# Masked cross attention: scores taken once with queries on partitions, exponentials turned by TensorE

## The chip, the cores and the metric

The kernel runs on one NeuronCore of a Trainium2 chip. The metric is the device time of one launch in microseconds. Before the change it is 2520.6 us (median of three runs, 2520.56 to 2532.2).

## The reference, cut to what matters

A small Perceiver of two layers over x [16, 64, 256] and a context [16, 1601, 256]: cross attention, an RWKV block, a mixture of experts; then cross attention with a mask and biases, differential attention, and a routed block. Only the second cross attention (layer `L1_xattn`) changes:

```python
q = split_heads(query @ Wq.T + bq)      # query: layer norm of x, 16 heads of 16
k = split_heads(key @ Wk.T + bk)        # key, value: the context, 1601 rows
v = split_heads(value @ Wv.T + bv)
scores = einsum('bhqd,bhkd->bhqk', q, k) / 4 + mask * -1e9
ctx = einsum('bhqk,bhkd->bhqd', softmax(scores), v)
x = x + ctx @ Wo.T + bo
```

## The kernel before

Six stages run one after another (A to F), with a barrier behind each. A and D are the two cross attentions, and both use `cross_attention`; D passes a mask. The work is cut into 32 groups: a group is one of the 16 batches and one half of its heads, eight heads as four pairs, j = 0 to 3. A pair has 32 channels and 128 columns of queries (64 of each head). The 1601 keys are 13 tiles of 128 (the last has 65) and four chunks of 512 (the last has 65).

Per group TensorE computes scores twice. First with queries on partitions (`score`, L536: 96 rows, since keys and queries are stacked as high and low fp32r halves; 16 matmuls into a ring of three PSUM banks), of which VectorE takes the maximum (`largest`; with a mask by the operation at L691, which adds the scaled mask). The negated maximum is turned onto rows (`turn_max`, L544) and placed in rows 96 to 127 of the stacked queries (`place_max`). Then again with keys on partitions (`scoresT`, L570: per key tile four matmuls of 128 rows, which subtract the maximum through these rows), with a mask one more matmul of 512 columns ahead of them (L566), ScalarE's exp from PSUM to SBUF (L648), and `values` (L584: 8 fp32 matmuls of 32 output rows per tile, four column groups, into `OUT`).

Keys are projected by `k_unit` (six fp32r matmuls per chunk) and values by `v_unit` (twelve per unit). ScalarE writes the high half of the keys (`k_hi`), VectorE the low half (`k_lo`), and 24 DMAs per group on SyncE's queue copy both into the stack `k_stack` (`keys`, L404); twelve more per batch bring the queries (`queries`, L391). GpSimd splits context, queries and mask.

The order is written out by hand: for each group g and key tile t TensorE does `scoresT(g, t)` and, at the slots in `K_SLOT`, `V_SLOT` and `S_SLOT`, a projection for the next batch or a score for group g+1; `values` run in pairs two tiles behind; `spread_sums` (L553) of group g-1 stands at slot 5, and VectorE's `finish` (L723 to L730) behind it. ScalarE and VectorE follow the same loops. Ahead of the attention lies the query stage (L231, L240), in which ScalarE fills rows of `k_stack` with ones (L247).

Of the kernel before, what the change touches and what calls it, by code (L numbers as in the profile page):

```python
# [8 lines left out]
F32 = mybir.dt.float32  # L9
# [61 lines left out]
class Chip:  # L71


    def __init__(self, nc):
        self.nc, self.used = nc, []

    def sem(self, name):
        self.used.append(self.nc.alloc_semaphore(name))
        return self.used[-1]
# [175 lines left out]
class Cross:  # L255


    def __init__(self, nc, chip, ctx, ctxT, tag):
        def sb(name, shape, dt=F32):
            return ctx.enter_context(nc.sbuf_tensor(name + tag, shape, dt))  # L260
        self.nc, self.ctxT = nc, ctxT
        self.raw = [sb(f"raw{i}", [P, HALVES, BANK]) for i in range(2)]
        self.xh, self.xl = sb("ctx_hi", [P, HALVES, KPAD], F32R), sb("ctx_lo", [P, HALVES, KPAD], F32R)
        self.stack = [sb(f"k_stack{i}", [P, 4, KPAD], F32R) for i in range(2)]
        self.raw_in = [chip.sem(f"raw_in{i}{tag}") for i in range(2)]
        self.ctx_hi_done, self.ctx_ready = chip.sem("ctx_hi_done" + tag), chip.sem("ctx_ready" + tag)

# [61 lines left out]
def cross_attention(nc, chip, cross, qT, attnT, wk, wv, bk, bv, mask, late, late_in, tag):  # L329
# [7 lines left out]
    with ExitStack() as ctx:  # L337
# [336 lines left out]
        def _(dve):  # L674
# [69 lines left out]
            for g in range(GROUPS):  # L744
                m, h = g // 2, g % 2
                for t in range(KT):
                    if t == MAX_SLOT and g + 1 < GROUPS:
                        negate(g + 1)
                        place_max(g + 1)
                    if t in K_SLOT and m + 1 < NB:  # L750
                        k_lo(m + 1, 4 * h + K_SLOT[t])
                    if t in S_SLOT and g + 1 < GROUPS:
                        for k in S_SLOT[t]:
                            largest(g + 1, k)
                    if t == SUM_SLOT and g:
                        finish(g - 1)
            finish(GROUPS - 1)

# [1026 lines left out]
def cross_stage(nc, chip, dram, layer, tag, mask):  # L1785

    with ExitStack() as ctx:
        def sb(name, shape, dt=F32):
            return ctx.enter_context(nc.sbuf_tensor(name + tag, shape, dt))
        qT, cross = sb("qT", [P, HALVES, TOK]), Cross(nc, chip, ctx, dram["ctxT"], tag)  # L1790
        bq, bk, bv = sb("bq", [P, HALVES]), sb("bk", [P, HALVES]), sb("bv", [P, HALVES])
        wo, bo, late_in = cross.raw[0][:, :, 0:D], cross.raw[1][0:1, 0, 0:D], chip.sem("late_in" + tag)
        w_step = chip.sem("w_step" + tag)
# [3 lines left out]
        with ExitStack() as ctx2:  # L1797
            split = [[ctx2.enter_context(nc.sbuf_tensor(n + tag, [P, HALVES, D], F32R))
                      for n in (w + "_hi", w + "_lo")] for w in ("wk", "wv")]
            with ExitStack() as ctx3:  # L1800
                y, yT, wq, wk, wv = [ctx3.enter_context(nc.sbuf_tensor(n + tag, [P, *s], F32)) for n, s in
                                     (("y", [NT, D]), ("yT", [HALVES, TOK]), ("wq", [HALVES, D]),
                                      ("wk", [HALVES, D]), ("wv", [HALVES, D]))]
                weights = [(t[:, :, :], chan(dram[layer + n])) for t, n in
                           ((wk, "Wk"), (wv, "Wv"), (wq, "Wq"))]
                if mask is not None:
                    weights += [(t[:, :], dram[layer + n]) for t, n in
                                ((bq, "bq"), (bk, "bk"), (bv, "bv"))]

                def early_loads(sp):  # L1810
                    cross.load(sp, 0, 0)
                    cross.load(sp, 0, 1)

                def early_splits(pool, loaded):
                    nc.gpsimd.memset(cross.xh[:, :, KEYS:KPAD].bitcast(F32), 0.0)
                    nc.gpsimd.memset(cross.xl[:, :, KEYS:KPAD].bitcast(F32), 0.0)
                    if mask is None:
                        for b in (bq, bk, bv):
                            nc.gpsimd.memset(b[:, :], 0.0)
                    pool.wait_ge(loaded, 16 * len(weights))  # L1820
                    for i, (w, (hi, lo)) in enumerate(zip((wk, wv), split)):
                        nc.gpsimd.tensor_copy(hi[:, :, :], w[:, :, :]).then_inc(w_step, 1)
                        pool.wait_ge(w_step, i + 1)
                        nc.gpsimd.tensor_tensor(lo[:, :, :], w[:, :, :], hi[:, :, :].bitcast(F32), ALU.subtract)
                    cross.split(pool, 0, 0)
                    cross.split(pool, 0, 1)
                norm_stage(nc, chip, chip.x, y, lambda h, q: yT[:, h, BANK * q:BANK * q + BANK], weights,
                           more_sync=early_loads, more_pool=early_splits, tag=tag)
                query_stage(nc, chip, cross, yT, wq, bq, 1.0 if mask is None else 0.25, qT, tag)
            cross_attention(nc, chip, cross, qT, qT, *split, bk, bv, mask, late, late_in, tag)  # L1830
        output_stage(nc, chip, qT, wo, None if mask is None else bo, late_in, len(late), tag)


# [82 lines left out]
```

## Time and profile before

| | |
|---|---|
| median of the runs | 2520.6 us |
| profiled execution | 2541.2 us |
| its span | 2539.4 us |
| TensorE busy, matmuls | 2204.7 us (87%) |
| VectorE / ScalarE / GpSimd busy | 1252.5 / 1011.8 / 614.2 us |
| mean granted clock of TensorE | 0.904 of 2.4 GHz |

The second cross attention's groups run from 1447.5 to 2317 us of the span. Busy times of TensorE overlap, since matmuls are pipelined: what an instruction costs its queue is read from its start to the next one's start. An fp32 matmul appears as two records, an fp32r matmul or a transpose as one. "x4" in a timeline is four records merged into one row; the time beside it runs from the first start to the last end.

### The profile page before, as it was taken

How to read it: one execution, taken by the hardware profiler on the slowest of the kernel's cores; microseconds unless marked ns; L12 is line 12 of the kernel's file. 1: busy time of each engine (PE TensorE's matmuls, PEld its weight loads, DVE VectorE, ACT ScalarE, POOL GpSimd, SP SyncE). 2: the span in 40 equal slices, each digit the busy share in tenths (PEclk: the TensorE clock that was granted, in tenths of full speed). 3: DMA queues.
4: the chain of work that ended last, by engine and by line, in shares of the span. 5: the costliest groups of instructions: out<-in, count | busy, mean ns of one | idle time of the engine just before them, and what ended most of it. 6: DMA issues, size and time to landing. Idle time of an engine off the chain costs nothing. (4 is left out here: it accounts for less than half of the span.)

```text
span 2539.4 us, 60278 instructions
## 1 busy us (share of the span) xinstructions
PE 2204.7 (87%) x24656; PEld 1817.9 (72%) x24656; DVE 1252.5 (49%) x2909; ACT 1011.8 (40%) x2180; POOL 614.2 (24%) x473
## 2 busy tenths in 40 slices
PE   5799999999999984194997799999999999998774
PEld 3687878878887862164896578888888888886453
DVE  3354544545445437823313345545545545543685
ACT  3244444444444423220322334444444444442581
POOL 3122222332222000021001353334444334410010
PEclk9799999999999957595998799999999999997766
DMA  4445555555555401005131555656556556540000
GB/s 119 114 120 132 137 120 133 126 137 136 131 126 128 105 17 41 0 1 190 67 119 50 136 125 140 145 135 146 139 137 145 136 139 144 139 98 23 13 1 23
DMA packets 166867, 267.52 MB, mean 105 GB/s; under 512 B 70713, under 2 KB 86210, under 8 KB 166594
## 3 DMA queue, kind: packets, MB, share of 16 engines
q1 hardware_dynamic: 166594, 263.66, 42.2%
q8 instruction: 198, 3.24, 0.6%
q14 instruction: 75, 0.61, 0.1%
HBM read 98.70 MB, written 1.05 MB: 39 GB/s over the span
## 5 line engine op out<-in xcount | busy, mean ns | idle before, releaser
L648 ACT ACTIVATE exp_d<-scoresT_d 128x512 f32<-128x512 f32 (+1 forms) x416 | 248.3, 597 | 274.2 <-PE scoresT_d L570 271.8
L691 DVE CUSTOM_DVE_ANT_0 scores_d<-scores_d,mask_scaled_d 128x512 f32<-128x512 f32 (+1 forms) x512 | 281.1, 600 | 145.8 <-PE scores_d L536 142.7
L695 DVE TENSOR_REDUCE max_parts_a<-scores_a 128x1 f32<-128x512 f32 (+1 forms) x512 | 263.4, 565 | 157.3 <-PE scores_a L536 157.3
L648 ACT ACTIVATE exp_a<-scoresT_a 128x512 f32<-128x512 f32 (+1 forms) x416 | 247.9, 596 | 214.5 <-PE scoresT_a L570 213.2
L570 PE MATMUL scoresT_a<-q_stack_a,k_stack_a 128*128 128x128 f32 (+1 forms) x1664 | 261.9, 283 | 0.9 <-DVE q_stack_a L712 0.9
L570 PEld LDWEIGHTS scoresT_d<-q_stack_d,k_stack_d 128*128 128x128 f32 (+1 forms) x1664 | 244.3, 187 | 24.1
L570 PEld LDWEIGHTS scoresT_a<-q_stack_a,k_stack_a 128*128 128x128 f32 (+1 forms) x1664 | 233.1, 198 | 28.3 <-issue 3.6
L570 PE MATMUL scoresT_d<-q_stack_d,k_stack_d 128*128 128x128 f32 (+1 forms) x1664 | 227.6, 259 | 0.0
L536 PE MATMUL scores_a<-k_stack_a,q_stack_a 96*128 96x512 f32 (+1 forms) x512 | 178.9, 404 | 40.2 <-issue 20.3
L679 DVE SCALAR_TENSOR_TENSOR k_lo_d<-project_d,bk_d,k_hi_d 128x512 fp32r<-128x512 f32 (+1 forms) x128 | 81.1, 635 | 258.0 <-ACT k_hi_d L631 258.0
L679 DVE SCALAR_TENSOR_TENSOR k_lo_a<-project_a,bk_a,k_hi_a 128x512 fp32r<-128x512 f32 (+1 forms) x128 | 80.8, 633 | 255.5 <-ACT k_hi_a L631 255.5
L284 POOL CAST ctx_hi_a<-raw_a 128x1024 fp32r<-128x1024 f32 x64 | 54.6, 853 | 586.4 <-PE project_a L110 504.7
L566 PE MATMUL scoresT_d<-pick_d,mask_hi_lo_d 128*128 128x512 f32 (+1 forms) x416 | 186.4, 448 | 0.8 <-issue 0.8
L536 PE MATMUL scores_d<-k_stack_d,q_stack_d 96*128 96x512 f32 (+1 forms) x512 | 171.2, 387 | 12.2 <-DMA k_stack_d<-k_hi_d 6.2
L284 POOL CAST ctx_hi_d<-raw_d 128x1024 fp32r<-128x1024 f32 x64 | 54.7, 855 | 470.1 <-PE project_d L110 379.1
L584 PE MATMUL values_a<-exp_a,v_a 128*32 128x64 f32 x6656 | 141.4, 228 | 1.5
L584 PEld LDWEIGHTS values_a<-exp_a,v_a 128*32 128x32 f32 x6656 | 107.0, 113 | 48.7 <-issue 39.2
L640 ACT ACTIVATE v_a<-project_a 128x512 f32<-128x512 f32 (+1 forms) x112 | 63.4, 566 | 187.6 <-PE project_a L110 187.4
L584 PE MATMUL values_d<-exp_d,v_d 128*32 128x64 f32 x6656 | 136.3, 222 | 1.7 <-ACT exp_d L648 0.2
L584 PEld LDWEIGHTS values_d<-exp_d,v_d 128*32 128x32 f32 x6656 | 102.6, 109 | 47.8 <-issue 38.7
L536 PEld LDWEIGHTS scores_a<-k_stack_a,q_stack_a 96*128 96x128 f32 x512 | 89.3, 199 | 55.8 <-issue 21.8
L108 PE MATMUL project_a<-wv_hi_a,ctx_hi_a 128*128 128x256 f32 (+1 forms) x416 | 126.4, 304 | 1.1 <-DVE k_lo_a L679 1.1
(370 smaller groups left out, 4849.6 us busy)
## 6 DMA issues: line engine op xcount, KB each, us to landing
k_stack_a<-k_hi_a SPq DMA_DIRECT2D x256, 128.0 KB
k_stack_d<-k_hi_d SPq DMA_DIRECT2D x256, 128.0 KB
raw_a<-in_ctxT SPq DMA_DIRECT2D x48, 512.0 KB, 4.2
raw_d<-in_ctxT SPq DMA_DIRECT2D x48, 512.0 KB, 5.0
w_c<-in_L_ffn_W SPq DMA_DIRECT2D x23, 1024.0 KB, 9.5
k_stack_a<-k_hi_a SPq DMA_DIRECT2D x256, 72.2 KB, 2.1
k_stack_d<-k_hi_d SPq DMA_DIRECT2D x256, 72.2 KB
k_stack_a<-k_lo_a SPq DMA_DIRECT2D x128, 128.0 KB
```

The lines of the kernel that those rows point to most:

```text
L108: nc.tensor.matmul(out, sh, mh, start=start, stop=False)
L284: self.nc.gpsimd.tensor_copy(self.xh[:, :, cols], self.raw[j % 2][:, :, 0:w]).then_inc(self.ctx_hi_done, 1)
L536: nc.tensor.matmul(SC[at % 3][:, 0:even(chunk)], qs[m % 2][0:96, 4 * h + j, :], stack[h][0:96, j, cols], start=True, stop=True).then_inc(s ...
L566: nc.tensor.matmul(bank[0:r, :], mb[m % 2][:, cols], pick[:, :].rearrange("p (a c) -> p a c", a=1).to_broadcast([P, 4, P]), start=True, st ...
L570: ins = nc.tensor.matmul(bank[0:r, P * j:P * j + P], stack[h][:, j, cols], qs[m % 2][:, 4 * h + j, :], start=not masked, stop=True, skip_g ...
L584: ins = nc.tensor.matmul(OUT[PW * j:PW * j + PW, h, T * a:T * a + T], v[m % 2][0:r, PAIRS * t + 4 * h + j, 16 * a:16 * a + PW], eT[at % RI ...
L640: nc.scalar.activation(pairs[:, :, 0::2, :], PJ[at % 2][0:r, 0:D * tiles].rearrange("p (i a c) -> p i a c", a=2, c=16), ACT.Copy).then_inc ...
L648: nc.scalar.activation(eT[at % RING][0:r, :], ST[at % 2][0:r, :], ACT.Exp).then_inc(exp_done, 1)
L679: nc.vector.scalar_tensor_tensor(kl[:, cols], PJ[at % 2][:, 0:even(chunk)], bk[:, h:h + 1], kh[:, cols].bitcast(F32), ALU.add, ALU.subtrac ...
L691: nc.vector.tensor_tensor_reduce(SC[at % 3][:, 0:w], SC[at % 3][:, 0:w], mf[m % 2][:, BANK * chunk:BANK * chunk + w], 1.0, NEG, ALU.add, A ...
L695: nc.vector.reduce_max(parts[:, j, chunk:chunk + 1], SC[at % 3][:, 0:w], AX.X).then_inc(score_free, 1)
```

## The change

Stage D gets its own function, `cross_by_rows`; stage A keeps `cross_attention`. In it:

- Keys are kept once in fp32 (`keys`, two buffers, one for each half), written by ScalarE or VectorE; `k_stack`, its fill with ones, the low halves, and the copies of keys and queries by DMA are gone.
- Scores are computed once per group, in four rounds (one per chunk) of four fp32 matmuls with 32 rows each, on partitions 32j, into four banks `SC[j]`. A round waits until VectorE has read all four banks of the round before.
- VectorE adds the mask and takes the maximum, and writes the masked scores to `maps` in SBUF. ScalarE takes exp over `maps` in place, four pairs by two pieces (1024 and 577 columns), with the negated maximum as bias. The mask matmul, `turn_max` and `place_max` are gone.
- TensorE turns `maps` tile by tile (four transposes of 128x128 per tile into two banks `TP`). ScalarE moves tiles 0 to 6 to SBUF, VectorE tiles 7 to 12. `values`, the sums and `finish` stay, the latter behind slot 9.
- Projections use one bank (`PJ`) in the steady state, three ahead of the first group. From slot 7 on VectorE keeps them, before that ScalarE.

The diff, cut to its core:

```diff
+K_AT = {1: 0, 4: 1, 7: 2, 10: 3}
+V_AT = [{3: 0, 6: 1, 9: 2, 12: 3}, {3: 4, 6: 5, 9: 6}]
+ROUND_AT = {0: 0, 2: 1, 4: 2, 6: 3}
+SUM_AT = 9
+LATE = 7
...
+            def scores(g, chunk):
+                m, h, w = g // 2, g % 2, cross.width(chunk)
+                if chunk == 0 and h == 0:
+                    pe.wait_ge(q_ready, m + 1)
+                wait_kept(pe, ("k", m, 4 * h + chunk))
+                after(pe, score_free, ROUND["score", g, chunk, 0])
+                for j in range(4):
+                    own = slice(PW * j, PW * j + PW)
+                    ins = nc.tensor.matmul(SC[j][:, 0:w], qs[m % 2][own, h, :],
+                                           keys[h][own, BANK * chunk:BANK * chunk + w], start=True, stop=True)
+                ins.then_inc(scored, 1)
+            def turn(g, t):
+                at, r = KT * g + t, rows(t)
+                if t in (0, CUT // P):
+                    pe.wait_ge(exp_done, 8 * g + (4 if t == 0 else 8))
+                wait_moved(pe, at - 2)
+                for j in range(4):
+                    ins = nc.tensor.transpose(TP[at % 2][0:r, P * j:P * j + P], maps[g % 2][:, j, P * t:P * t + r],
+                                              chip.ident)
+                ins.then_inc(turned, 1)
...
+            for g in range(GROUPS):
+                m, h = g // 2, g % 2
+                for t in range(KT):
+                    if t == 0 and g:
+                        values(g - 1, KT - 1)
+                    turn(g, t)
+                    if t in ROUND_AT and g + 1 < GROUPS:
+                        scores(g + 1, ROUND_AT[t])
+                    if t in K_AT and m + 1 < NB:
+                        k_unit(m + 1, 4 * h + K_AT[t])
+                    if t in V_AT[h] and m + 1 < NB:
+                        v_unit(m + 1, V_AT[h][t])
+                    if t == SUM_AT and g:
+                        spread_sums(g - 1)
+                    if t and t % 2 == 0:
+                        values(g, t - 2)
+                        values(g, t - 1)
...
+            def exp(g, piece, j):
+                cols, b = (slice(CUT, KEYS) if piece else slice(0, CUT)), g % 2
+                act.wait_ge(max_ready, g + 1)
+                nc.scalar.activation(maps[b][:, j, cols], maps[b][:, j, cols], ACT.Exp,
+                                     bias=low[:, b, j:j + 1]).then_inc(exp_done, 1)
...
+            for g in range(GROUPS):
+                m, h = g // 2, g % 2
+                for t in range(LATE):
+                    move(g, t)
+                    if t == 0 and g:
+                        keep_out(g - 1)
+                    if t in K_AT and m + 1 < NB:
+                        keep_k(m + 1, 4 * h + K_AT[t])
+                    if t in V_AT[h] and m + 1 < NB:
+                        keep_v(m + 1, V_AT[h][t])
+                if g + 1 < GROUPS:
+                    for i in range(8):
+                        exp(g + 1, i // 4, i % 4)
...
+                nc.vector.tensor_tensor_reduce(
+                    maps[b][:, j, cols], SC[j][:, 0:w], mf[m % 2][:, cols] if masked else none[:, 0:w], 1.0, NEG,
+                    ALU.add, ALU.max, parts[:, j, chunk:chunk + 1]).then_inc(score_free, 1)
...
+            for g in range(GROUPS):
+                m, h = g // 2, g % 2
+                for t in range(KT):
+                    if t >= LATE:
+                        move(g, t)
+                    if t in ROUND_AT and g + 1 < GROUPS:
+                        for j in range(4):
+                            largest(g + 1, ROUND_AT[t], j)
+                        if ROUND_AT[t] == 3:
+                            negate(g + 1)
+                    if t >= LATE and t in K_AT and m + 1 < NB:
+                        keep_k(m + 1, 4 * h + K_AT[t])
+                    if t >= LATE and t in V_AT[h] and m + 1 < NB:
+                        keep_v(m + 1, V_AT[h][t])
+                    if t == SUM_AT and g:
+                        finish(g - 1)
...
-        qT, cross = sb("qT", [P, HALVES, TOK]), Cross(nc, chip, ctx, dram["ctxT"], tag)
+        qT, cross = sb("qT", [P, HALVES, TOK]), Cross(nc, chip, ctx, dram["ctxT"], mask is None, tag)
...
-            cross_attention(nc, chip, cross, qT, qT, *split, bk, bv, mask, late, late_in, tag)
+            attend = cross_attention if mask is None else cross_by_rows
+            attend(nc, chip, cross, qT, qT, *split, bk, bv, mask, late, late_in, tag)
```

## Rows read from the trace of the kernel before

**Rows 1.** Table of stretches (start:end, length, busy per engine, granted clock, DMA)

```profile
1447.50:1500.40 52.90, 44.26 (x489) 37.75 (x490) 19.55 (x55) 17.81 (x31) 21.87 (x14) 0.88 0.57 138
1500.40:2291.50 791.10, 785.74 (x10351) 667.08 (x10351) 414.99 (x1276) 354.06 (x621) 307.26 (x191) 1.00 0.58 136
```

**Rows 2.** TensorE's timeline (start, duration, engine, line): sums of two groups

```profile
1856.56 0.41 PE L553 MATMUL scores_d<-out_copy_d,const 128*128 128x64 f32 x2
...
2268.49 0.29 PE L553 MATMUL scores_d<-out_copy_d,const 128*128 128x64 f32 x1
```

**Rows 3.** TensorE's timeline, steady group: its sums and work behind it

```profile
1801.31 0.63 PE L553 MATMUL scores_d<-out_copy_d,const 128*128 128x64 f32 x4
...
1803.88 0.68 PE L536 MATMUL scores_d<-k_stack_d,q_stack_d 96*128 96x512 f32 x2
1804.48 0.65 PE L584 MATMUL values_d<-exp_d,v_d 128*32 128x64 f32 x32
1805.07 0.50 PE L566 MATMUL scoresT_d<-pick_d,mask_hi_lo_d 128*128 128x512 f32 x1
1805.41 0.56 PE L570 MATMUL scoresT_d<-q_stack_d,k_stack_d 128*128 128x128 f32 x4
1805.80 0.45 PE L108 MATMUL project_d<-ctx_hi_d,wk_hi_d 128*128 128x512 f32 x1
...
1807.25 0.39 PE L536 MATMUL scores_d<-k_stack_d,q_stack_d 96*128 96x512 f32 x1
```

**Rows 4.** TensorE's instructions by form, one group (xcount | busy us, mean ns)

```profile
L570 PE MATMUL scoresT_d<-q_stack_d,k_stack_d 128*128 128x128 f32 x48 | 6.7, 262 | 0.0
...
L536 PE MATMUL scores_d<-k_stack_d,q_stack_d 96*128 96x512 f32 x13 | 5.0, 421 | 0.0
```

**Rows 5.** Timeline and stretch: transposes in the differential stage; plain fp32 matmuls

```profile
2485.53 3.67 PE L1547 MATMUL ht_e<-const,gained_e 128*128 128x128 f32 x16 [5.16 <-DVE gained_e L1539]
...
2485.50:2489.20 3.70, 3.67 (x16) 3.27 (x16) 1.78 (x3) 1.80 (x3) 0.00 (x0) 0.50 0.00 0
...
1399.05 4.46 PE L231 MATMUL q_d<-yT_d,wq_d 128*128 128x512 f32 x10
```

**Rows 6.** VectorE's timeline: two masked reads, and finish of a group

```profile
1439.05 0.73 DVE L691 CUSTOM_DVE_ANT_0 scores_d<-scores_d,mask_scaled_d 128x512 f32<-128x512 f32 x1
...
1439.70 0.73 DVE L691 CUSTOM_DVE_ANT_0 scores_d<-scores_d,mask_scaled_d 128x512 f32<-128x512 f32 x1
...
1802.32 0.95 DVE L723 RECIPROCAL rec_d<-scores_d 128x128 f32<-128x128 f32 x1
...
1804.35 0.70 DVE L691 CUSTOM_DVE_ANT_0 scores_d<-scores_d,mask_scaled_d 128x512 f32<-128x512 f32 x1
```

**Rows 7.** Instructions by form: a copy on VectorE, exps on ScalarE

```profile
L1673 DVE COPY dT_e<-dt_e 128x512 f32<-128x512 f32 x16 | 11.0, 686 | 2.4 <-PE dt_e L1607 2.4
...
L648 ACT ACTIVATE exp_d<-scoresT_d 128x512 f32<-128x512 f32 x384 | 229.4, 597 | 268.2 <-PE scoresT_d L570 265.9
...
L961 ACT ACTIVATE e_b<-e_b 128x1024 f32<-128x1024 f32 x6 | 6.3, 1057 | 23.3 <-DVE e_b L881 20.0 <-DVE e_b L898 3.0
```

**Rows 8.** Timeline ahead of the first group [idle before <-releaser]

```profile
1394.10 11.51 ACT L247 ACTIVATE k_stack_d<-const 32x1602 fp32r<-32x1602 f32 x8 [0.27 <-PEq L131]
...
1403.54 0.75 DVE L240 TENSOR_SCALAR qT_d<-q_d,bq_d 128x512 f32<-128x512 f32 x1 [0.97 <-PE q_d L231]
...
1423.20 0.48 PE L108 MATMUL project_d<-ctx_hi_d,wk_hi_d 128*128 128x512 f32 x1
...
1430.10 1.26 ACT L631 ACTIVATE k_hi_d<-project_d,bk_d 128x512 fp32r<-128x512 f32 x2 [6.56 <-DMA k_stack_d<-k_hi_d]
...
1447.54 0.76 PE L566 MATMUL scoresT_d<-pick_d,mask_hi_lo_d 128*128 128x512 f32 x1 [0.83 <-issue]
```

**Rows 9.** Table of stretches, first cross attention: TensorE waits, and afterwards

```profile
565.80:569.20 3.40, 1.99 (x58) 1.53 (x57) 0.35 (x2) 1.62 (x4) 2.93 (x5) 1.00 0.68 152
569.20:572.70 3.50, 3.12 (x13) 3.02 (x14) 0.69 (x1) 0.00 (x0) 0.39 (x1) 0.51 0.53 119
```

More of the change, by code:

```diff
@@ L255, with __init__ @@
 class Cross:
-    def __init__(self, nc, chip, ctx, ctxT, tag):
+    def __init__(self, nc, chip, ctx, ctxT, stacked, tag):
         def sb(name, shape, dt=F32):
@@ L263, in __init__ @@
         self.xh, self.xl = sb("ctx_hi", [P, HALVES, KPAD], F32R), sb("ctx_lo", [P, HALVES, KPAD], F32R)
-        self.stack = [sb(f"k_stack{i}", [P, 4, KPAD], F32R) for i in range(2)]
+        self.stack = [sb(f"k_stack{i}", [P, 4, KPAD], F32R) for i in range(2)] if stacked else []
         self.raw_in = [chip.sem(f"raw_in{i}{tag}") for i in range(2)]
@@ L755, in _, with unit_order @@
                     if t == SUM_SLOT and g:
+                        finish(g - 1)
+            finish(GROUPS - 1)
+K_AT = {1: 0, 4: 1, 7: 2, 10: 3}
[3 more added lines that the diff above has]
+LATE = 7
+FIRST_UNITS = 15
+def unit_order():
+    order = [("k", 0, k) for k in range(4)] + [("v", 0, u) for u in range(7)] + [("k", 0, k) for k in range(4, 8)]
+    for m in range(1, NB):
+        for h in range(HALVES):
+            for t in range(KT):
+                if t in K_AT:
+                    order.append(("k", m, 4 * h + K_AT[t]))
+                if t in V_AT[h]:
+                    order.append(("v", m, V_AT[h][t]))
+    return {unit: i for i, unit in enumerate(order)}
```

260 lines of the change are left out of this document (added).

## The prediction

> **What bounds the kernel now.** I read four views, from coarse to fine. The table of stretches first: over the long stretch of the second cross attention TensorE is busy 785.74 of 791.10 us at a granted clock of 1.00, while VectorE has 414.99 and ScalarE 354.06 us of work [rows 1]. So nothing but TensorE's own queue sets the pace there, and a change pays by what it takes out of that queue, as long as no other engine becomes the next one. Second, two marks of the same matmul (the one that spreads the sums, slot 5 of a group): a pair of groups from 1801.31 to 1856.56 us takes 55.25 us, and fifteen groups from 1856.56 to 2268.49 take 411.93 us, so 27.46 us per group [rows 2, 3]. Third, the groups of TensorE instructions of one group: 48 full transposed-score matmuls beside four narrow ones, so 52 over 13 key tiles, each tile led by one mask matmul; 12 score matmuls of 512 columns (the window catches 13) and four narrow ones [rows 4]. Fourth, the timeline, for what each costs from its start to the next start, since the busy times overlap [rows 3]. From 1805.41 to 1805.80 four transposed scores take 0.39. A key unit, six matmuls of 512 columns, takes 1.45 (1805.80 to 1807.25), 0.24 each. A mask matmul, also 512 columns, takes 0.34 behind values (1805.07 to 1805.41) and I count 0.23 elsewhere. A pair of values tiles takes 0.59 (1804.48 to 1805.07), of which the records need 0.65-0.22=0.43 and the change of tile shape about 0.15.
>
> **What leaves TensorE, per group.** Mask: 7 x 0.23 + 6 x 0.34 = 3.65 us. Transposed scores: 13 x 0.39 = 5.1. First scores: two of them with the values switch behind take 0.60 (1803.88 to 1804.48), so 12 x 0.29 plus four narrow ones at 0.12 = 4.0. Turning of the maximum: about 0.35. Together 13.1 us.
>
> **What comes in.** (a) 52 transposes of 128x128 fp32. The trace has them in the differential stage: 16 in 3.67 us, of which the last one's own 0.42 is latency, so 0.217 us each, at a clock of 0.50 [rows 5]. It never shows one at the full clock. A plain fp32 matmul of 512 columns at the full clock takes (4.46-0.59)/9 = 0.43 us per record [rows 5], 0.84 ns a column, and the transpose at half clock 1.7 ns a column: the same cycles. I take 0.108 each, 5.6 us per group; the other end is 0.217, 11.3 us. (b) The mask matmul was also what stood between values and the next 128-row work; its extra 0.11 now falls on a turn, six times: 0.7. (c) Scores with 32 rows each on four row groups. fp32 has two records of 0.43 per matmul. If the four run beside one another, a round takes 0.86; if they don't, 3.44. Nothing in the trace splits rows. The nearest row splits columns: 32 values records take 0.43 us [rows 3], 14 ns apiece, while 64 columns at 0.84 ns are 54 ns alone, so four groups do run side by side there. I take 0.86 plus 0.2 for changing shape: 3 x 1.06 + 0.4 for the narrow round = 3.6. Together 9.9 us.
>
> The Trainium skill (TensorE: Matmul & The Clock Gate, Part 3) gives 3.07 times for four row tiles with 512 columns, not four times. No row here shows it. By it a round would be 8 x 0.43 / 3.07 = 1.12, and the sum some 6 us later.
>
> So TensorE's need falls from 27.46 to 24.3 us per group. Whether it gets that depends on the others.
>
> **VectorE's new chain.** Each round writes all four score banks, and the next round waits until VectorE has read all four: the ring of three single banks is gone. One masked read starts 0.65 after the one before [rows 6], so four take 2.6 and the hand-overs 0.2. It now writes maps to SBUF. The nearest PSUM to SBUF row, a copy of 512 columns, took 0.686 [rows 7], less than the 0.73 of a read as it is, so I keep 0.65 (0.70 would cost 5 us in all, 0.60 gain as much). TensorE's filler between rounds 0 and 1 is turn, key unit, turn: 0.43+1.45+0.43 = 2.3, so about 0.5 us of wait. Between 1 and 2 it is values, turn, value unit, turn: 0.74+0.43+1.43+0.43 = 3.0, and between 2 and 3 as much: covered. A group then runs: values and turn 0.75, round 0 to 1.8, round 1 at 4.65, round 2 at 8.75, round 3 done at about 13.2. From there VectorE does the narrow reads and the new maximum (1.2 us), then moves 7 to 12 at 0.69 each (that copy again), two or three kept units, and the finish of the old group, 1802.32 to 1804.35 = 2.03 [rows 6]. The finish is queued ahead of move 10, and turn 12 waits for move 10: about 10.2 us after round 3, while TensorE's own queue has brought it there after 10. Both ends together: 26.1 us with four value units, 24.6 with three; 25.4 on average, a saving of 2.05 per group. VectorE's work is some 17 us per group, so as a sum it does not bind; only its order does.
>
> **ScalarE** has 7 moves (0.597 each, by the exp of the same tile), 8 exps over SBUF (four of 1024 columns, which took 1.057 [rows 7], some 0.94 from start to start; four of 577, 0.54 in proportion), kept units and the output: about 14 of 25 us. The exps start when the maximum is ready, 1.2 to 2 us after round 3, and need 5.9; the next group's first turn comes 11 us after round 3. If that cover went, every us over it would be paid in each group.
>
> **Queues.** SyncE loses 24 key copies per group and 12 query copies per batch, so context and mask loads are never behind them. The mask load now waits for a read of group 2m-3, two groups ahead of its use. GpSimd loses two of its three mask steps and the query splits, and keeps the splits of the context; it only gets freer.
>
> **Ahead of the first group** and in its first two. Today: the ones' fill on ScalarE runs 1394.10 to 1405.61 and ends the query stage, whose last VectorE step is over at 1403.54+0.75 = 1404.3: 1.3 us go [rows 8]. Then ScalarE waits 6.56 us until the copies have left k_hi, and the first transposed score starts at 1447.54 [rows 8]. After: TensorE does keys, values and rounds without those waits. Key unit 4 starts at 1423.20 today [rows 8]; with four rounds ahead of it (3.6 us) it ends near 1428; ScalarE then has a table load, six exps and four kept units before the bank wait lets the first turn go, near 1436.4: 11 us earlier. The stretch from 1447.5 to 1500.4 lasts 52.90 at clock 0.88 [rows 1] for 1.4 groups, some 39 us at the steady pace. That excess of 14 is copies and splits arriving late; I give 10 of it back. The last two groups have no projections: there the reads chain costs 1 us more and the last group's moves 1 less.
>
> **Sum.** 30 x 2.05 = 61.5; + 10 + 11 + 1.3 = 84. Waits of 0.5 us may cost some clock: in the first cross attention a stretch with 1.99 of 3.40 us busy was followed by one at 0.51 [rows 9]. Each such 3.4 us stretch loses 1.7; I take off 8 us for five of them. Net 76. The profiled execution took 2541.2 us (span 2539.4), the median is 2520.6: 2465 there, x 2520.6/2541.2 = 2445 us.
>
> **Rivals.**
> A. *The four row groups do not run side by side.* A round costs 3.44+0.2, 2.6 more, three times per group, with VectorE waiting for the last: +8 per group, about 2690. Against it: the values rows.
> B. *The clock falls.* The turns are 5.6 of 25 us, with small waits around. Every transpose in the trace ran at 0.50 [rows 5], although always after an idle stretch. If a share f of the time were at half clock a group would last 25.4/(1-f/2); at f = 0.2 it eats the gain. At a third it is 30.5 per group and about 2600. That is the slower side, decided at f = 0.2. A transpose that stays at 0.217 ends near the same place (+5 per group).
> The skill's page on TensorE (Part 4, PE-mode transpose) says that transposes do not count as activity for the clock; if so, this rival is the one it speaks for. The trace can't tell, because all of its transposes follow a wait.
> C. *Lock step.* Round and read alternate with later hand-overs, or the finish pushes turns 10 to 12: 1.5 us more per group, 2490 to 2500; the gain mostly gone.
> D. *Better.* VectorE's order doesn't bind and TensorE gets its 24.3: 2410.
>
> **How the numbers follow.** Forecast 0.54, A 0.08, B 0.16, C 0.14, D 0.08. 8 in 10: from 2405 (D and the low bounds) to 2570, which leaves out A and most of B. This kernel can be told from no change at about 0.5%, 12.6 us. Faster: forecast, D and most of C, 0.74; same 0.05; slower 0.21.
>
> **What would show it.** A turn as four transposes 0.107 apart at clock 1.00; a round's eight records within 0.9 us; marks of the sums 25.4 apart on average; waits of TensorE for the masked reads near 0.5 per group, for the last moves near nothing; the first turn near 1436. Wrong if the clock row of the long stretch shows less than 0.9, if a round takes 2 us or more, or if ScalarE's exps end after the group's last turn.

## The result and the profile after

The changed kernel takes 2461.2 us (median of four runs, 2453.0 to 2464.2) against 2520.6; the ratio is 0.9753, with a 95% interval of 0.9712 to 0.9794. The profiled execution took 2461.6 us, its span is 2459.8.

The lengths in this part are read from TensorE's timeline in the same way for every kernel: the start of the first transpose (or first transposed score) of groups 0, 2 and 30, and of the last of all. A turn is the four transposes of one key tile. The pace is the difference between groups 2 and 30, divided by 28.

| second cross attention, us | before | after | difference |
|---|---|---|---|
| end of the query stage's last VectorE step to group 0 | 43.8 | 34.3 | -9.5 |
| groups 0 and 1 | 67.1 | 52.6 | -14.5 |
| groups 2 to 29 (pace) | 768.1 (27.43) | 721.4 (25.77) | -46.7 |
| group 30 to the last turn | 31.5 | 33.0 | +1.4 |

Together 69.3 us. The two profiled executions differ by 79.6: 11.4 more stand ahead of this stage, in code that is the same (the last step of the query stage ends at 1404.3 before [rows 8] and at 1392.9 here), and 1.1 comes back behind it. The profiled execution before was 20.6 us above its median, the one after 0.4 above its own. That is why the medians, 59.4 us apart, and not the two profiles are the measure. Of the 20 us, 11 stand ahead of the stage; no run shows where the others lie, and the 69.3 may hold some of them.

The table of stretches of the changed kernel, the columns as in [rows 1]:

```profile
1437.00:1490.00 53.00, 50.59 (x728) 38.51 (x727) 30.39 (x92) 27.93 (x42) 15.24 (x10) 1.00 0.18 48
1490.00:2240.00 750.00, 711.72 (x10524) 548.28 (x10524) 462.82 (x1344) 386.82 (x577) 198.10 (x130) 1.00 0.16 44
```

In the long stretch the clock stays at 1.00, as before, TensorE is busy 95% where it was 99% [rows 1], the moved data fall from 136 to 44 GB/s, and VectorE and ScalarE have more to do. Groups 0 and 1 ran at a lower clock before than they do now (before, then after):

```profile
1447.50:1514.80 67.30, 58.55 (x712) 49.97 (x712) 28.21 (x84) 24.42 (x42) 26.90 (x19) 0.91 0.56 133
1427.16:1479.70 52.54, 50.91 (x714) 38.84 (x714) 30.25 (x89) 27.80 (x41) 19.78 (x15) 0.96 0.22 61
```

At a mean clock of 0.91 some 6 of the 67 us are lost, at 0.96 some 2 of the 53: by this estimate about 4 of the 14.5 us come from the clock. The marks of the sums, to hold against [rows 2]:

```profile
1500.50 0.44 PE L979 MATMUL scores_d<-out_copy_d,const 128*128 128x64 f32 x3
...
2170.16 0.44 PE L979 MATMUL scores_d<-out_copy_d,const 128*128 128x64 f32 x3
```

26 groups in 669.66 us are 25.76 us each, where it was 27.46. One group of TensorE's timeline, to hold against [rows 3]:

```profile
1804.58 0.66 PE L970 MATMUL turn_d<-const,maps_d 128*128 128x128 f32 x4
1804.99 0.48 PE L108 MATMUL project_d<-ctx_hi_d,wk_hi_d 128*128 128x512 f32 x1
...
1806.47 0.60 PE L970 MATMUL turn_d<-const,maps_d 128*128 128x128 f32 x4
1807.00 0.65 PE L992 MATMUL values_d<-mapsT_d,v_d 128*32 128x64 f32 x32
...
1811.88 0.66 PE L970 MATMUL turn_d<-const,maps_d 128*128 128x128 f32 x4
1812.91 0.65 PE L970 MATMUL turn_d<-const,maps_d 128*65 128x128 f32 x4 [0.38 <-DVE mapsT_d L1125]
...
1815.71 0.65 PE L970 MATMUL turn_d<-const,maps_d 128*128 128x128 f32 x4
1816.29 1.14 PE L960 MATMUL scores_d<-keys_d,q_rows_d 32*128 32x512 f32 x8
1817.36 0.66 PE L970 MATMUL turn_d<-const,maps_d 128*128 128x128 f32 x4
1817.78 0.48 PE L108 MATMUL project_d<-ctx_hi_d,wk_hi_d 128*128 128x512 f32 x1
...
1820.32 1.14 PE L960 MATMUL scores_d<-keys_d,q_rows_d 32*128 32x512 f32 x8 [0.46 <-DVE max_parts_d L1097]
```

A turn is 0.41 to 0.42 (1804.58 to 1804.99, 1817.36 to 1817.78), a little over 0.10 for each of its four transposes at the full clock. A round takes 1.07 (1816.29 to 1817.36). Its eight records run in two passes of four: in the trace four start at 1816.29 and four at 1816.83, so a pass takes 0.53 or 0.54. The turn ahead of a round takes 0.58 (1815.71 to 1816.29), and the one ahead of values 0.53 (1806.47 to 1807.00): there is a cost on the way in as well. Round 1 waits 0.46 for VectorE's reads, and turn 12 waits 0.38. These idle times are counted from the modelled end of the last record. From start to start turn 12 comes 1.03 behind turn 11 (1811.88 to 1812.91) where a turn otherwise needs 0.41, so it is held for 0.62. The waits of TensorE over 26.4 groups (engine, line, who was waited for, total us, times, longest):

```profile
PE turn_d L970 <- DVE mapsT_d L1125: 12.2, 27, 0.7
PE scores_d L960 <- DVE max_parts_d L1097: 10.8, 24, 0.5
PE values_d L992 <- DVE mapsT_d L1125: 2.5, 13, 0.2
```

So about 0.45 us per group in front of turn 12 and, where it is named so, 0.45 in front of round 1. From start to start, as a mean over groups 2 to 29, turn 12 is held for 0.69 us and round 1 for 0.53. VectorE's timeline beside it:

```profile
1810.31 0.95 DVE L1132 RECIPROCAL rec_d<-scores_d 128x128 f32<-128x128 f32 x1
...
1812.17 0.69 DVE L1125 COPY mapsT_d<-turn_d 128x512 f32<-128x512 f32 x1
...
1817.64 0.69 DVE L1097 CUSTOM_DVE_ANT_0 maps_d<-scores_d,mask_scaled_d 128x512 f32<-128x512 f32 x1 [1.94 <-PE scores_d L960]
...
1818.26 0.69 DVE L1097 CUSTOM_DVE_ANT_0 maps_d<-scores_d,mask_scaled_d 128x512 f32<-128x512 f32 x1
```

Reads start 0.61 apart (0.65 in [rows 6]); the finish holds VectorE from 1810.31 to 1812.17, and the copy behind it is move 10, for which turn 12 waits. The lead-in, to hold against [rows 8]:

```profile
1392.15 0.75 DVE L240 TENSOR_SCALAR qT_d<-q_d,bq_d 128x512 f32<-128x512 f32 x1 [0.96 <-PE q_d L231]
...
1399.52 4.27 POOL L909 TENSOR_SCALAR mask_scaled_d<-mask_scaled_d 128x1601 f32<-128x1601 f32 x1 [5.72 <-DMA mask_scaled_d<-in_mask]
1401.08 1.14 PE L960 MATMUL scores_d<-keys_d,q_rows_d 32*128 32x512 f32 x8
...
1403.83 0.69 DVE L1097 CUSTOM_DVE_ANT_0 maps_d<-scores_d,mask_scaled_d 128x512 f32<-128x512 f32 x1 [7.06 <-POOL mask_scaled_d L909]
...
1406.51 1.14 PE L960 MATMUL scores_d<-keys_d,q_rows_d 32*128 32x512 f32 x8 [2.67 <-DVE max_parts_d L1097]
...
1427.16 1.08 PE L970 MATMUL turn_d<-const,maps_d 128*128 128x128 f32 x4 [5.69 <-ACT keys_d L1035]
```

The first round (1401.08) was through TensorE at 1402.15, the mask was ready at 1403.79. VectorE had been idle for 7.06 us by then, but for most of it there was nothing to read: a read starts 0.28 behind its round in the steady groups (1817.36 to 1817.64), so the mask held the first one for 1.4 us. TensorE stood still for 2.67 us ahead of round 1, and for 5.69 more until ScalarE had kept all units between its exps.

### The profile page after: what moved, and what is told of

It is laid out like the page before. It is cut to its first block and busy times, and to the rows that moved or that the text cites. A ratio compares the mean times of both kernels' runs of the same rounds, so it can differ in the third digit from the quotient of the medians.

```text
span 2459.8 us, 59466 instructions
## 1 busy us (share of the span) xinstructions
PE 2107.4 (86%) x24688; PEld 1673.6 (68%) x24688; DVE 1299.2 (53%) x2980; ACT 1040.3 (42%) x2131; POOL 499.6 (20%) x409
## 5 line engine op out<-in xcount | busy, mean ns | idle before, releaser
L1097 DVE CUSTOM_DVE_ANT_0 maps_d<-scores_d,mask_scaled_d 128x512 f32<-128x512 f32 (+1 forms) x512 | 263.6, 572 | 212.1 <-PE scores_d L960 205.1
L970 PE MATMUL turn_d<-const,maps_d 128*128 128x128 f32 (+1 forms) x1664 | 258.4, 282 | 21.5 <-DVE mapsT_d L1125 15.6
L970 PEld LDWEIGHTS turn_d<-const,maps_d 128*128 128x128 f32 (+1 forms) x1664 | 183.6, 142 | 79.3 <-issue 30.0
L1049 ACT ACTIVATE mapsT_d<-turn_d 128x512 f32<-128x512 f32 x224 | 129.7, 595 | 230.8 <-PE turn_d L970 230.7
L1054 ACT ACTIVATE maps_d<-maps_d,neg_max_d 128x1024 f32<-128x1024 f32 (+1 forms) x256 | 222.0, 952 | 1.9 <-DVE neg_max_d L1104 1.9
L536 PE MATMUL scores_a<-k_stack_a,q_stack_a 96*128 96x512 f32 (+1 forms) x512 | 177.4, 399 | 36.5 <-DMA k_stack_a<-k_hi_a 20.7
L1125 DVE COPY mapsT_d<-turn_d 128x512 f32<-128x512 f32 x192 | 129.9, 686 | 75.5 <-PE turn_d L970 75.2
L960 PE MATMUL scores_d<-keys_d,q_rows_d 32*128 32x512 f32 (+1 forms) x1024 | 124.9, 556 | 20.5 <-DVE max_parts_d L1097 19.2
L992 PEld LDWEIGHTS values_d<-mapsT_d,v_d 128*32 128x32 f32 x6656 | 102.7, 109 | 58.3 <-issue 43.8
L992 PE MATMUL values_d<-mapsT_d,v_d 128*32 128x64 f32 x6656 | 136.9, 222 | 3.4 <-DVE mapsT_d L1125 3.4
L536 PEld LDWEIGHTS scores_a<-k_stack_a,q_stack_a 96*128 96x128 f32 x512 | 88.5, 198 | 51.7 <-DMA k_stack_a<-k_hi_a 23.0
```

Source lines behind the costliest of these rows:

```text
L536: nc.tensor.matmul(SC[at % 3][:, 0:even(chunk)], qs[m % 2][0:96, 4 * h + j, :], stack[h][0:96, j, cols], start=True, stop=True).then_inc(s ...
L960: ins = nc.tensor.matmul(SC[j][:, 0:w], qs[m % 2][own, h, :], keys[h][own, BANK * chunk:BANK * chunk + w], start=True, stop=True)
L970: ins = nc.tensor.transpose(TP[at % 2][0:r, P * j:P * j + P], maps[g % 2][:, j, P * t:P * t + r], chip.ident)
L992: ins = nc.tensor.matmul(OUT[PW * j:PW * j + PW, h, T * a:T * a + T], v[m % 2][0:r, PAIRS * t + 4 * h + j, 16 * a:16 * a + PW], mT[at % RI ...
L1049: nc.scalar.activation(mT[at % RING][0:r, :], TP[at % 2][0:r, :], ACT.Copy).then_inc(moved_act, 1)
L1054: nc.scalar.activation(maps[b][:, j, cols], maps[b][:, j, cols], ACT.Exp, bias=low[:, b, j:j + 1]).then_inc(exp_done, 1)
```

## The experiments

All edits are to the changed kernel unless said otherwise; the diffs are cut to their core. Each ratio is to runs of the kernel before that were made together with the experiment. The median of those was 2525.2 us for experiments 1 to 4, 2520.1 for 5 to 8 and 2533.0 for 9 to 11, so across these sets ratios and paces can be compared, times only roughly.

**1. The row groups.** The queries of a pair are padded with zeros to 128 rows (the diff leaves out the padding itself).

```diff
-                    ins = nc.tensor.matmul(SC[j][:, 0:w], qs[m % 2][own, h, :],
-                                           keys[h][own, BANK * chunk:BANK * chunk + w], start=True, stop=True)
+                    ins = nc.tensor.matmul(SC[j][:, 0:w], qs[m % 2][:, j, h, :],
+                                           keys[h][:, BANK * chunk:BANK * chunk + w], start=True, stop=True)
```

> The changed kernel, but each score matmul has 128 rows (queries padded with zeros in the 96 rows of the other pairs) instead of 32 rows on a row group of its own. Same outputs, same number of matmul records. Theory (four row groups run side by side, rival A wrong): a round, 1.08 us from its start to the next start in the changed kernel, becomes 8 records x 0.43 = 3.4 us, so +2.4 us three times a group and some 0.4 for the narrow round: groups go from 25.8 to about 33.4 us, 31 of them, so about 2461 + 236 = 2697 us. Rival (the packing brings nothing, the round's cost lies elsewhere): no change, 2461.

Measured: 2685.5 us, ratio 1.065 (1.060 to 1.070) to the kernel before; the pace is 33.12. TensorE's timeline:

```profile
1822.46 0.66 PE L977 MATMUL turn_d<-const,maps_d 128*128 128x128 f32 x4
1822.95 3.60 PE L967 MATMUL scores_d<-keys_d,q_rows_d 128*128 128x512 f32 x8
1826.39 0.60 PE L977 MATMUL turn_d<-const,maps_d 128*128 128x128 f32 x4
```

The same eight records take 3.44 us instead of 1.07, so side by side they run 3.2 times as fast, and the whole edit costs 7.35 us per group. Without the row groups the change would have lost 160 us. The turn ahead of the round now takes 0.49 instead of 0.58. So 0.09 of its extra 0.16 goes with the change of shape; the other 0.07 stays without one, and no run shows its cause. The stretch table shows the clock as it was:

```profile
1500.00:2300.00 800.00, 772.62 (x8675) 556.89 (x8674) 385.05 (x1124) 323.46 (x483) 204.75 (x156) 1.00 0.14 39
```

**2. The transposes.** Each is written as a plain fp32 matmul with the identity.

```diff
-                    ins = nc.tensor.transpose(TP[at % 2][0:r, P * j:P * j + P], maps[g % 2][:, j, P * t:P * t + r],
-                                              chip.ident)
+                    ins = nc.tensor.matmul(TP[at % 2][0:r, P * j:P * j + P], maps[g % 2][:, j, P * t:P * t + r],
+                                           chip.ident, start=True, stop=True)
```

> The changed kernel with the 52 transposes per group written as plain fp32 matmuls with the identity (two records each instead of one). Theory (a transpose costs one record of 0.107 us at the full clock): a turn goes from 0.43 to 0.86 us, +5.6 us per group, of which 0.5 to 0.9 fall into waits that exist already: +4.9 x 31 = +150, about 2611 us. Rival B in what is left of it (transposes hold the clock down, plain matmuls would not): clock and time no worse than with transposes, 2461 or below.

Measured: 2615.1 us, ratio 1.037 (1.033 to 1.042); pace 30.72, 4.95 more. A turn has eight records:

```profile
1817.96 1.05 PE L970 MATMUL turn_d<-const,maps_d 128*128 128x128 f32 x8
```

and the clock of the stretch is no different from that with transposes:

```profile
1500.00:2300.00 800.00, 797.46 (x10700) 667.27 (x10699) 420.03 (x1209) 358.55 (x522) 197.52 (x130) 1.00 0.15 41
```

The pace is that of the theory, +4.9, and the rival falls. A turn ahead of a projection went from 0.41 to 0.91, so a transpose costs about half of what the same tile costs as an fp32 product. In this mix, where turns are a quarter of TensorE's time, they do not hold the clock down; what they do alone was not tried.

**3. The mask matmul, in the kernel before.** It is left out of the second scores, which so lack the mask; the maximum still has it.

```diff
-                if masked:
-                    nc.tensor.matmul(bank[0:r, :], mb[m % 2][:, cols],
-                                     pick[:, :].rearrange("p (a c) -> p a c", a=1).to_broadcast([P, 4, P]),
-                                     start=True, stop=False, skip_group_check=True)
```

> The kernel before without the 13 mask matmuls per group (the second scores then go without the mask, the maximum still has it). Theory 1 (TensorE's queue alone sets the pace, as my sum has it): 3.65 us per group less, 27.4 to 23.8, so about 2520 - 115 = 2405 us. Theory 2 (the copies of the keys by DMA stand close behind, as in the first cross attention, which has no mask matmul and still takes 26.8 us per group): 27.4 to 26.8, about 2500 us, with waits for k_stack in the trace.

Measured: 2502.4 us, ratio 0.990 (0.987 to 0.993); pace 26.33. Taking 3.7 us of work per group from TensorE gave 1.1. Of TensorE's waits between 1500 and 2180 us, 26 groups, those for the copies sum to 16 us:

```profile
PE scores_d L536 <- DMA k_stack_d<-k_hi_d: 16.0, 13, 1.9
```

That is 0.6 per group. Another part shows in the timeline (L566 is the transposed scores here, L579 values, L536 the first scores):

```profile
1813.28 0.65 PE L579 MATMUL values_d<-exp_d,v_d 128*32 128x64 f32 x32
...
1816.04 0.56 PE L566 MATMUL scoresT_d<-q_stack_d,k_stack_d 128*128 128x128 f32 x4
1816.44 0.67 PE L536 MATMUL scores_d<-k_stack_d,q_stack_d 96*128 96x512 f32 x2
1817.04 0.65 PE L579 MATMUL values_d<-exp_d,v_d 128*32 128x64 f32 x32
1817.62 0.66 PE L566 MATMUL scoresT_d<-q_stack_d,k_stack_d 128*128 128x128 f32 x4
1818.20 0.50 PE L536 MATMUL scores_d<-k_stack_d,q_stack_d 96*128 96x512 f32 x1
```

Away from values four transposed scores take 0.40 (1816.04 to 1816.44), behind values 0.58 (1817.62 to 1818.20). Each instruction's time from its start to the next start, summed by line over groups 2 to 29 and divided by 28, went from 3.70 to nothing for the mask matmuls, from 5.27 to 7.16 for the transposed scores, from 3.95 to 4.43 for the first scores, and up by 0.2 for the projections. So 2.6 us per group are missing, and the trace gives three parts of them:

- Waits, which stand inside these sums: together 0.1 us per group before and 1.1 now, 0.6 of it for the copies.
- The change of shape behind values: six times a group 0.19 on the short matmuls (0.58 where they took 0.39 behind a mask matmul), 1.1 us. On the mask matmul it had cost 0.11 (0.34 for 0.23), which my 3.65 counted as if it left too. So the mask matmul, 512 columns long, had covered 0.08 each time, and the other 0.11 only moved.
- The clock: six short stretches of these 28 groups ran at half of it, some 0.4 us per group.

These lengths come from one profile of each kernel. The first cross attention, whose code is the same in both, has a pace of 26.39 in one and 25.91 in the other, so the 1.1 is good to a few tenths only.

At the end of the stage waits and clock cost more. From group 30 on the stage took 46.8 us where it took 31.5. TensorE's wait for the copies, and then the last groups' stretch (this kernel, and the kernel before):

```profile
2231.96 0.80 PE L536 MATMUL scores_d<-k_stack_d,q_stack_d 96*128 96x512 f32 x1 [3.19 <-DMA k_stack_d<-k_hi_d]
```

```profile
2228.00:2274.50 46.50, 43.31 (x508) 37.21 (x498) 14.55 (x44) 14.66 (x26) 0.00 (x0) 0.52 0.14 33
2282.90:2314.30 31.40, 30.42 (x524) 25.64 (x520) 14.15 (x44) 14.57 (x26) 0.00 (x0) 1.00 0.19 43
```

That takes back 15 of the 31 us that the pace gave. Both theories fall as I put them: TensorE's work is not simply shorter by what is taken out, and the waits for the copies are a quarter of what is missing in the pace. That the time is the 2500 of theory 2 is luck: the pace is better than its 26.8, and the end of the stage takes the difference.

**4. VectorE's finish behind move 12.**

```diff
-                    if t == SUM_AT and g:
+                    if t == KT - 1 and g:
                         finish(g - 1)
```

> The changed kernel with VectorE's finish of the old group moved from slot 9 to behind move 12. Theory: turn 12 waits about 0.4 us per group for move 10, because the finish (2 us) is queued ahead of it; that wait goes, groups 25.77 to about 25.4 us, about 2449 us. Rival: the finish now delays the bank of the sums, which round 0 of the next group needs, or the kept value unit, by more than it gives: 2461 to 2475 us with a new wait of round 0.

Measured: 2463.5 us, ratio 0.977 (0.974 to 0.980); pace 26.05. The two kinds of groups part: those with three value units went from 24.85 to 24.68, those with four from 26.68 to 27.41. VectorE's and TensorE's timelines of the latter:

```profile
1818.65 0.69 DVE L1119 COPY v_d<-project_d 128x512 f32<-128x512 f32 x1 [0.57 <-PE project_d L110]
1819.26 0.95 DVE L1132 RECIPROCAL rec_d<-scores_d 128x128 f32<-128x128 f32 x1
...
1821.69 0.69 DVE L1097 CUSTOM_DVE_ANT_0 maps_d<-scores_d,mask_scaled_d 128x512 f32<-128x512 f32 x1 [0.49 <-PE scores_d L960]
```

```profile
1820.35 1.14 PE L960 MATMUL scores_d<-keys_d,q_rows_d 32*128 32x512 f32 x8 [0.34 <-DVE rec_d L1132]
...
1824.37 1.14 PE L960 MATMUL scores_d<-keys_d,q_rows_d 32*128 32x512 f32 x8 [0.45 <-DVE max_parts_d L1097]
```

The wait of turn 12 is gone, but the kept value unit and the finish now stand ahead of the reads of round 0, round 0 waits for the bank of the sums, and round 1 for reads that start late. The rival holds; the wait was moved, not removed.

**5. The last values tile behind round 0.**

```diff
-                    if t == 0 and g:
-                        values(g - 1, KT - 1)
                     turn(g, t)
                     if t in ROUND_AT and g + 1 < GROUPS:
                         scores(g + 1, ROUND_AT[t])
+                    if t == 0 and g:
+                        values(g - 1, KT - 1)
```

> The changed kernel with the last values tile of the old group put behind round 0 instead of ahead of the first turn, so that TensorE has 0.4 us more to do between rounds 0 and 1. Theory: the wait of round 1 for VectorE's four reads, 0.5 us per group, shrinks to 0.1: groups 25.77 to about 25.35 us, about 2449 us. Rival: the wait only looks like one for the reads (the profile also names ScalarE's keys) and stays: 2461 us.

Measured: 2446.6 us, ratio 0.971 (0.967 to 0.976); pace 25.35, as expected: the wait of round 1 was one for the reads. The only wait of TensorE left in the list is that of turn 12, with the same 12.2 us as in the changed kernel.

**6. Edits 4 and 5 together.**

> The two moves together (finish behind move 12, last values behind round 0). Theory: they are two separate waits, so they add: groups about 24.95 us, about 2436 us. Rival: one wait hands over to the other, 2449 us.

Measured: 2465.6 us, ratio 0.979 (0.975 to 0.983); pace 25.99. Edit 4 takes back what edit 5 gave, nearly all of it in the groups with four value units (27.67, where edit 5 alone has 26.46):

```profile
PE scores_d L960 <- DVE max_parts_d L1097: 16.6, 13, 1.3
PE scores_d L960 <- DVE rec_d L1132: 14.9, 27, 0.6
```

Neither of the two outcomes that I wrote down came about.

**7. The first cross attention by the new function too.** It has no mask; VectorE adds zeros.

```diff
-            attend = cross_attention if mask is None else cross_by_rows
+            attend = cross_by_rows
```

> The changed kernel with the first cross attention by the new function as well (without a mask, VectorE adds zeros). Theory (what the new form saves is mostly the copies of the keys and the second scores, not the mask): the first stage's groups go from 26.8 to 25.8 us, its lead-in and its clock dips go as in the second, some 30 + 25 us: about 2405 us. Rival (the gain is the mask matmul's, which the first stage never had): the first stage gains nothing or loses, 2461 us or more.

Measured: 2417.4 us, ratio 0.960 (0.955 to 0.964). The diff leaves out one line that sets up the first stage's buffers for it. The first stage's first turn (experiment) and first transposed score (changed kernel, with the wait for the copies behind it):

```profile
68.15 0.66 PE L970 MATMUL turn_a<-const,maps_a 128*128 128x128 f32 x2 [5.68 <-ACT keys_a L1035]
```

```profile
78.17 1.09 PE L570 MATMUL scoresT_a<-q_stack_a,k_stack_a 128*128 128x128 f32 x4 [0.88 <-DVE q_stack_a L712]
82.05 0.79 PE L536 MATMUL scores_a<-k_stack_a,q_stack_a 96*128 96x512 f32 x1 [2.79 <-DMA k_stack_a<-k_hi_a]
```

By the same lengths the first stage gives 10.0 us ahead of group 0, 12.1 in groups 0 and 1, 7.1 in groups 2 to 29 (26.01 to 25.76) and 11.7 from group 30 on. The last of these goes with the clock. The stretch from group 30 on, in the changed kernel and in this one:

```profile
870.80:915.10 44.30, 43.25 (x503) 37.22 (x496) 13.63 (x28) 14.67 (x26) 0.00 (x0) 0.51 0.12 28
841.00:874.20 33.20, 25.87 (x529) 18.98 (x525) 18.66 (x53) 14.98 (x24) 0.00 (x0) 1.00 0.01 3
```

Where both forms end at the full clock, in the second stage, the new one is no faster there (33.0 for 31.5). So the gain is there without a mask matmul to remove, and the clock dips go, as I had written; but most of it lies at the ends of the stage and not in the pace. Of the 7.1 us in the pace not all is sure: over groups 2 to 29 this stage, its code unchanged, took from 725.4 to 738.8 us in the ten profiles that have the old form, and 721.2 here. The pace of 26.8 that I wrote down for this stage was a mean over all its groups, the slow first ones included.

**8. A values pair next to a round.** On top of edits 4 and 5.

```diff
                         scores(g + 1, ROUND_AT[t])
                     if t == 0 and g:
                         values(g - 1, KT - 1)
+                    if t == 4:
+                        values(g, t - 2)
+                        values(g, t - 1)
...
-                    if t and t % 2 == 0:
+                    if t and t % 2 == 0 and t != 4:
                         values(g, t - 2)
                         values(g, t - 1)
```

> As the two moves together, and in slot 4 the values pair stands right behind round 2 instead of behind the key unit. Theory (each change of the array's shape costs 0.15 us, the term I mis-sized): one change less per group, 24.95 to 24.8, 2432 us. Rival (row groups to column groups costs as much as each alone): no difference to the two moves together.

Measured: 2452.8 us, ratio 0.973 (0.968 to 0.978), and a pace of 25.84 against 25.99: 0.15 per group for one change of shape less. TensorE's waits are the same in both traces (16.6 us for the reads, 14.8 and 14.9 for the bank of the sums), so the 0.15 is not a wait. The medians are 13 us apart, of which this pace explains 4; the four times lie between 2442 and 2457. The absolute times written down assumed that edits 4 and 5 add, which they don't.

**9. Both stages, with edit 5.**

> Both cross attentions by the new function, and in both the last values tile of the old group behind round 0. Theory (the two gains are in different places and add; per group 25.76 to 25.35 in each stage): 2417 - 2 x 30 x 0.41 = 2393 us. Rival (without a mask the first stage's VectorE is no quicker, but its groups are held by something else): 2405 us.

Measured: 2393.2 us, ratio 0.944 (0.941 to 0.947); pace 25.33 and 25.34. The theory holds.

**10. Move 10 on ScalarE behind the exps, with edit 5.**

```diff
+ACT_TILES, DVE_TILES = [0, 1, 2, 3, 4, 5, 6, 10], [7, 8, 9, 11, 12]
...
                     for i in range(8):
                         exp(g + 1, i // 4, i % 4)
+                move(g, 10)
...
-                    if t >= LATE:
+                    if t in DVE_TILES:
                         move(g, t)
```

> The changed kernel with the last values tile behind round 0, and move 10 given from VectorE to ScalarE, behind the exps. Theory (turn 12 waits 0.45 us per group for move 10, which stands behind the finish on VectorE, and nothing else does): the wait goes without moving the finish, groups 25.35 to 24.95, 2447 - 12 = 2435 us. Rival (ScalarE's exps end too late, some 11 us after round 3, and move 10 comes no earlier): 2447 us or more, the wait now named with ScalarE.

Measured: 2446.8 us, ratio 0.966 (0.962 to 0.970); pace 25.03. What is left of the wait stands in half of the groups only (1500 to 2100 us), and is now one for ScalarE, as the rival had it:

```profile
PE turn_d L973 <- ACT mapsT_d L1052: 6.0, 12, 0.5
```

The pace gained 0.31 (8.8 us), the last groups lost 3.1 (32.4 to 35.5). The four times lie between 2438 and 2456, and the ratio's interval overlaps that of experiment 5 (0.967 to 0.976), so the time can't tell such a difference.

**11. Both stages, with both edits.**

> Both cross attentions by the new function with both edits (values behind round 0, move 10 on ScalarE). Theory: all gains add, 2393 - 25 = 2368 us. Rival: move 10 brings nothing, 2393 us.

Measured: 2380.2 us, ratio 0.939 (0.936 to 0.942), 13 us below experiment 9; pace 25.01 and 25.03. This is the fastest version: 6.1% below the kernel before, where the change itself has 2.5%. Move 10 gives half of what I expected: over groups 2 to 29 9 us per stage (0.31 per group where I had 0.4), of which the last groups take back 2.4 in the first stage and 3.1 in the second.

## Why the prediction was right

The time (2445, range 2405 to 2570) holds the 2461, 16 us above the forecast. By its own steps:

- **What comes in.** The transposes: 0.41 a turn where I had 0.43. The other end, 0.217 each, is out by the timeline after. The row groups: a round of 1.07 where I had 1.06, and experiment 1 shows 3.44 without them. Rival A is out. The 0.2 in it has the right size, but it is no single change of shape: each of the two passes of four records takes 0.53 or 0.54, and one record of 128 rows takes 0.43 (3.44 / 8, experiment 1).
- **The shape of the array.** This term was mis-sized. I took 0.2 per round; it is 0.2 inside the round and 0.16 on the turn ahead (0.58 against 0.42), four times a group: 0.65 us. By experiment 1 about half of the 0.16 is the change of shape. Experiment 8 measures one change by itself: 0.15. The 0.11 that I put on each turn behind values isn't there (0.41); it stands on the turn ahead of them (0.53), so that sum held.
- **VectorE's chain.** Round 1 is held for 0.53 where I had 0.5. For turn 12 I expected waits "near nothing", with VectorE at 10.2 us after round 3 and TensorE after 10; it is held for 0.69 from start to start. Place and reason were right, the finish ahead of move 10, and so was the order of size: in the group shown turn 12 starts 10.5 us after round 3 (1802.38 to 1812.91), and TensorE alone would have been there after 9.9 (1811.88 + 0.41). Reads are 0.04 quicker than in [rows 6], which paid part of this back. ScalarE's exps hold nothing up: no wait for them stands in the list.
- **The pace**, from all that: 25.77 instead of 25.40, over the 28 groups 46.7 us saved instead of 57.4. Less the two waits (1.2 where the forecast left 1.1) TensorE's own need is 24.55 us where I had 24.3. With four value units a group takes 26.68 (I had 26.1), with three 24.85 (24.6).
- **Groups 0 and 1**: 14.5 us for 10 + 2 x 2.05 = 14.1. The size was right, the reason only in part: I put the slow start down to copies and splits that arrive late, but the clock of 0.91 holds about 4 us of it.
- **The lead-in**: 9.5 us for 11 + 1.3. The prediction has no term for the mask, which held the first read for 1.4 us.
- **The end**: 1.4 us worse, where I had 1 more against 1 less.
- **The clock**: I took 8 us off for it; the row of the long stretch says 1.00, with waits of about half a microsecond twice a group. Rival B is out for this mix. The Trainium skill (TensorE: Matmul & The Clock Gate, Part 4) spoke for it with transposes that don't count as activity for the clock. This mix does not bear that out: turns are a quarter of TensorE's time, and the clock of the stretch is 1.00 with transposes and with plain matmuls (experiment 2). Transposes by themselves were not run. The Trainium skill's 3.07 times for four row tiles (TensorE: Matmul & The Clock Gate, Part 3) stands beside 3.2 measured (experiment 1).

In sum 84 - 8 = 76 were forecast. The stage gave 69.3 by the two profiles; the medians moved by 59.4. Part of the nearness is luck: the 8 us taken off for a clock that did not fall stand against the 11 us that the pace came short. Without them the forecast would have been about 2437, 24 us off.

The weakest step of the reasoning does not show in the number. I wrote that a change pays by what it takes out of TensorE's queue. Experiment 3 takes 3.7 us per group out of it and gets 1.1, because the change of shape behind values does not leave with the mask matmul, because waits, for the copies above all, stood close behind (I had priced them at nothing in the steady groups), and because the clock fell. In the change these costs went away with their causes (no transposed scores, no copies), and the sum had a term for the shape behind values, so the sum over the whole exchange came out; the same prices for the mask alone would have been wrong by 2.6 us per group.

## What to carry to other kernels

An engine that is busy 99% of a stretch says what bounds it now, not how much a shorter queue gives: a cost such as the change of shape moves on to the next instruction, other waits stand close behind, and with them the clock can fall (experiment 3). Compare the granted clock of the ends of a stage too: in experiment 7 its 11.7 us from group 30 on came with a clock of 1.00 for 0.51. Matmuls of 32 rows in fp32, packed on four row groups with a bank each, ran three times as fast as one after the other, but a change of shape cost about 0.15 us (experiment 8), so put work of one shape side by side. Where a round of matmuls writes all banks at once, count TensorE's filler until the reads are over, and do not queue a long chain (the finish) ahead of a copy that TensorE waits for; moving the chain to the end of the group only moves the wait.

## What the runs showed of the hardware

- Four fp32 matmuls of 32 rows and 512 columns on four row groups took 1.07 us, in two passes of 0.53 or 0.54; the same on all 128 rows took 3.44, eight records of 0.43 one after the other (experiment 1).
- A turn of four 128x128 fp32 transposes took 0.41 us at the full clock, as fp32 products with the identity 0.91 (experiment 2). At half the clock a transpose took 0.217 [rows 5].
- VectorE's masked read that writes to SBUF starts 0.61 us after the one before; writing back to PSUM it was 0.65 [rows 6].
- With two waits of about half a microsecond per group the clock stayed at 1.00 over 750 us. In experiment 3 TensorE waited 3.19 us for a copy near 2230 us, and the last groups ran at 0.52.
- Code that no edit touched took up to 22 us more or less from one execution to the next: the second query stage's last step ended at 1404.3 us before, at 1392.9 in the changed kernel and at 1382.5 in experiment 3.
